# Three maximum units in a row behind the transposed scores: a change to the order of TensorE's work in the first attention

## The chip, the cores and the metric

The kernel runs on one core of a Trainium2 chip. The metric is the device time of one execution in microseconds; the time before is the median of three runs, 1740.41 us. A profile comes from one further execution, which took 1746.19 us and whose instructions span 1744.5 us.

## The reference

The program computes two transformer layers in sequence, each an attention and a mixture of experts behind layer norms with residual adds. All values are float32. Only the first attention bears on the change. Cut to what matters:

```python
# z: (2, 1024, 128), 16 heads of 64
q = z @ wq @ fcq_w + fcq_b
k = z @ wk @ fck_w + fck_b
v = z @ wv @ fcv_w + fcv_b
scores = einsum('bihd,bjhd->bhij', q, k) / 8
attn = softmax(scores, axis=-1)      # over all 1024 keys
out = einsum('bhij,bjhd->bihd', attn, v)
return out.reshape(b, n, 1024) @ fco_w + fco_b
```

For each of 2 x 16 heads there are 1024 x 1024 scores; the softmax takes a maximum over the keys of each query, an exponential, and a sum.

## The kernel before

The first attention (`l0_attention`) works through 16 steps. A step is one pair of heads of one batch element, with all its 1024 queries and keys. It loops over 8 key tiles of 128 keys (kt 0 to 7). For each key tile TensorE computes the transposed scores, with keys on the partitions and queries along the free axis, in two blocks of 512 queries: `("ST", kt, 0)` and `("ST", kt, 1)`. Each is 4 matmuls (lines 683 and 684, two per head, into one PSUM pair). ScalarE takes the exponential of each pair into a `prob` tile (line 550). GpSimd adds the `prob` tiles up over kt into `psum_k` (lines 502 and 507). TensorE multiplies the `prob` tiles with the values and accumulates in PSUM over kt: `("PV", kt - 1, j)`, one key tile behind the scores (line 656, 4 matmuls per block j, 8 for both).

The maxima that a step subtracts are found one step ahead. For step n + 1 TensorE also computes plain scores with queries on the partitions, in 16 units `("s", x)`: unit x takes query tile x // 2 and half x % 2 of the keys, for both heads (lines 629 and 631, two matmuls that sit in different row groups of the array). VectorE reduces each such pair to its row maxima (line 571). After the sixteenth, VectorE joins the two halves (`mmax`, line 575), unit `m` transposes the result on TensorE (line 635), VectorE makes a row of it (line 580), and SyncE moves it by DMA into the operand `q2` of the next step.

Other units: `q` projects the next step's queries (line 620, read on ScalarE, line 517, and VectorE, line 565). `l`, `r`, `n` and `g` finish the step before: `l` sums `psum_k` over partitions on TensorE (line 640; VectorE copies it out on line 584), `r` is a reciprocal on VectorE (line 587) whose result goes out by DMA and comes back spread over the partitions as `rb`, `n` is the product `on` of `ut` and `rb` on VectorE (line 591), and `g` is the output projection on TensorE (line 645) with an add on VectorE behind it (line 595).

The order is written out by hand. `step_script(n)` makes one list, and every engine walks it:

```python
for kt in range(TT):
    out += [("ST", kt, 0), ("ST", kt, 1)]
    out += [("UNIT",) + u for u in AFTER_SCORES.get(kt, []) if u in has]
    if kt or n:
        out += [("PV", kt - 1, 0), ("PV", kt - 1, 1)]
    out += [("UNIT",) + u for u in AFTER_VALUES.get(kt, []) if u in has]
```

PSUM holds two banks for the accumulating `pv` and a ring of three pairs (`RING = 3`, two banks each). Every ST block and every unit but `r` and `n` takes the next pair of the ring in the order of the script; PV takes none. Before TensorE writes a pair it waits for the reader of the tile three places back in that order, either the exponential (semaphore `exp_done`) or the reading unit (`read`):

```python
def await_buffer(pe, kind, at):
    i = turn[(kind, at)]
    if i >= RING:
        before, count = tiles[i - RING]
        pe.wait_ge(exp_done if before == "ST" else read, count + 1)
```

So in an ordinary key tile the ring goes ST 0, ST 1, s, s, s, and the reader that each waits for is that of, in turn, the last tile's first s, its second s, its third s, this tile's ST 0 and this tile's ST 1. The instructions of an engine run in their order in the script. The sixteenth step has no next one and so no `q`, `s` or `m` units; the sixteen units for the first step run ahead of the loop.

Of the kernel before, what the change touches and what calls it, by code (L numbers as in the profile page):

```python
# [302 lines left out]
def step_units(k_next, k_done):  # L303
# [5 lines left out]

AFTER_SCORES = {  # L310
    0: [("q", 0), ("q", 1)],
    1: [("s", 0), ("s", 1)], 2: [("s", 3), ("s", 4)], 3: [("s", 6), ("s", 7)], 4: [("s", 9), ("s", 10)],
    5: [("s", 12), ("s", 13)], 6: [("s", 15)],
}
AFTER_VALUES = {
    1: [("s", 2), ("l", 0)], 2: [("s", 5)], 3: [("s", 8), ("r", 0)], 4: [("s", 11), ("n", 0)], 5: [("s", 14), ("g", 0)],
    6: [("m", 0)],
}


# [1765 lines left out]
```

## Time and profile before

| | |
|---|---|
| median of 3 runs | 1740.41 us (1734.69 to 1742.39) |
| the profiled execution | 1746.19 us, span 1744.5 us |
| TensorE matmul busy | 1435.8 us (82%) |
| VectorE busy | 997.7 us (57%) |
| ScalarE busy | 795.7 us (46%) |
| GpSimd busy | 899.7 us (52%) |

The steps of the first attention lie between about 109 and 835 us of the span. In the views, PE is TensorE's matmul, PEld its weight load, DVE VectorE, ACT ScalarE, POOL GpSimd and SP SyncE. A line of the timeline gives the start, the duration, the engine and line, the operation, what it writes and reads with the shapes, and how many instructions are merged; in brackets stands the idle time of the engine before it and what ended it. Matmuls are pipelined, so the next one's start says more than a duration does.

### The profile page before, as it was taken

The page shows a single profiled execution, that of the slowest core. Times are in us where ns is not written, and L with a number is a line of the kernel's source. Part 1 is how long each engine was busy: PE and PEld are TensorE (multiplying, and loading weights), DVE is VectorE, ACT ScalarE, POOL GpSimd, SP SyncE. Part 2 cuts the span into 40 slices and gives each one's busy share as a digit, 9 for nine tenths or more (in the row PEclk, how much of TensorE's full clock was granted, in tenths as well). Part 3 has the DMA queues.
Part 4 walks back from the last instruction along what each step waited for, and adds up shares of the span by engine and source line. Part 5 has one row for each costly group of instructions (what it writes and reads, how often), then busy time and mean ns, then how long its engine had stood idle before and what let it go on. Part 6 is the DMA issues. An engine that isn't in the chain of part 4 may idle for free. (4 is left out here: it accounts for less than half of the span.)

```text
span 1744.5 us, 19190 instructions
## 1 busy us (share of the span) xinstructions
PE 1435.8 (82%) x6318; PEld 816.1 (47%) x6318; DVE 997.7 (57%) x1646; ACT 795.7 (46%) x1152; POOL 899.7 (52%) x703
## 2 busy tenths in 40 slices
PE   4679999999999999996458646988788885399998
PEld 3534444444444444442336423444344443277776
DVE  3165666666665656651635556655455514488777
ACT  2224444444443434432225342555455463388787
POOL 0227777777776767787225322445444232054444
PEclk9579999999999999998579887998889886599999
DMA  3000000000000000000144122111211102402200
GB/s 78 4 1 2 14 14 14 14 14 14 14 13 14 14 13 14 14 14 25 37 98 96 58 69 53 25 25 38 55 32 25 26 3 109 86 13 49 60 6 6
DMA packets 34562, 55.28 MB, mean 32 GB/s; under 512 B 10009, under 2 KB 15522, under 8 KB 33762
## 3 DMA queue, kind: packets, MB, share of 16 engines
q1 hardware_dynamic: 34482, 54.26, 12.5%
q8 instruction: 44, 0.72, 0.2%
q14 instruction: 36, 0.29, 0.1%
HBM read 37.73 MB, written 1.44 MB: 22 GB/s over the span
## 5 line engine op out<-in xcount | busy, mean ns | idle before, releaser
L507 POOL TENSOR_TENSOR psum_k<-psum_k,prob 128x1024 f32<-128x1024 f32 x192 | 463.3, 2436 | 85.5 <-ACT prob L550 85.5
L550 ACT ACTIVATE prob<-pair 128x1024 f32<-128x1024 f32 x256 | 251.3, 1027 | 422.0 <-PE pair L684 421.8
L571 DVE TENSOR_REDUCE mx<-pair 128x2 f32<-128x1024 f32 x256 | 303.9, 1221 | 114.6 <-PE pair L631 114.6
L1611 DVE CUSTOM_DVE_ANT_0 l_banks<-l_banks,causal 128x128 f32<-128x128 f32 (+7 forms) x256 | 189.9, 781 | 147.9 <-PE l_banks L1640 146.5
L656 PE MATMUL pv<-prob,c_all 128*64 128x512 f32 x1024 | 247.7, 605 | 0.0
L1527 ACT ACTIVATE l_prob<-l_banks 128x1024 f32<-128x1024 f32 (+7 forms) x256 | 156.3, 655 | 169.1 <-PE l_banks L1659 169.0
L683 PE MATMUL pair<-qq,ak 128*128 128x512 f32 x512 | 223.0, 436 | 5.6 <-DMA q<-scratch_shift 4.6
L684 PE MATMUL pair<-q,kb 128*128 128x512 f32 x512 | 204.5, 399 | 0.0
L1804 POOL TENSOR_TENSOR silu_rest<-silu,silu_lead 128x512 fp32r<-128x512 f32 x72 | 113.1, 1570 | 150.6 <-ACT silu_lead L1848 150.6
L1640 PE MATMUL l_banks<-l_kk,l_qq 128*128 128x512 f32 (+3 forms) x384 | 126.7, 424 | 70.6 <-DMA l_qq<-l_head 65.3
L1573 POOL TENSOR_SCALAR_AFFINE_SELECT l_prob<-l_prob 128x128 f32<-128x128 f32 x256 | 71.7, 295 | 192.2 <-ACT l_prob L1527 191.1
L1876 DVE TENSOR_TENSOR silu<-silu,gb 128x512 f32<-128x512 f32 x128 | 139.2, 1089 | 27.7 <-ACT silu L1855 25.7
L1640 PEld LDWEIGHTS l_banks<-l_kk,l_qq 128*128 128x128 f32 x384 | 75.2, 222 | 135.5 <-issue 90.8
L683 PEld LDWEIGHTS pair<-qq,ak 128*128 128x128 f32 x512 | 97.5, 190 | 83.5 <-issue 32.5
L502 POOL TENSOR_TENSOR psum_k<-prob 128x1024 f32<-128x1024 f32 x32 | 75.4, 2377 | 112.9 <-ACT prob L550 112.9
L1659 PE MATMUL l_banks<-l_qq,l_kk 128*128 128x512 f32 (+3 forms) x384 | 122.1, 410 | 4.2 <-DVE l_mx L1611 3.6
L629 PE MATMUL pair<-ak,qq 64*128 64x512 f32 x256 | 112.4, 486 | 6.2 <-DVE mx L571 5.3
L565 DVE SCALAR_TENSOR_TENSOR q<-pair,q_bias,qq 64x512 fp32r<-64x512 f32 x64 | 44.4, 759 | 125.1 <-ACT qq L517 125.1
L656 PEld LDWEIGHTS pv<-prob,c_all 128*64 128x64 f32 x1024 | 62.2, 136 | 109.1 <-issue 77.7
L631 PE MATMUL pair<-kb,qq 64*128 64x512 f32 x256 | 112.4, 486 | 0.0
L684 PEld LDWEIGHTS pair<-q,kb 128*128 128x128 f32 x512 | 97.8, 191 | 22.2 <-issue 4.1
L1848 ACT CAST silu_lead<-silu 128x512 fp32r<-128x512 f32 x144 | 88.9, 620 | 28.8 <-DVE silu L1876 28.8
(221 smaller groups left out, 2265.6 us busy)
## 6 DMA issues: line engine op xcount, KB each, us to landing
gb<-scratch_gates SPq DMA_DIRECT2D x8, 2048.0 KB, 14.1
rb<-scratch_sums SPq DMA_DIRECT2D x32, 256.0 KB
l_qq<-qr SPq DMA_DIRECT2D x8, 768.0 KB, 5.6
whole_r<-in_w SPq DMA_DIRECT2D x2, 2304.0 KB, 11.4
l_kk<-l_head SPq DMA_DIRECT2D x64, 64.0 KB, 2.0
l_qq<-l_head SPq DMA_DIRECT2D x64, 64.0 KB, 2.0
x<-in_x SPq DMA_DIRECT2D x4, 256.0 KB, 6.6
whole_r<-in_up SPq DMA_DIRECT2D x1, 1024.0 KB, 5.2
```

The source lines that it names most:

```text
L507: nc.gpsimd.tensor_tensor(total[:, h, :], total[:, h, :], prob[kt % 4][:, h, :], ALU.add).then_inc(summed, 1)
L550: nc.scalar.activation(prob[kt % 4][:, :, ts(j, BLK)], buffer("ST", at)[:, :, :], ACT.Exp, scale=D0 ** -0.5).then_inc(exp_done, 1)
L571: nc.vector.reduce_max(mx[:, x % 2, :, x // 2], buf[:, :, :], AX.X).then_inc(read, 1)
L656: ins = nc.tensor.matmul(pv[D0 * h:D0 * (h + 1), ts(j, BLK)], m.c_all[:, TT * (s // PAIRS) + kt, :], prob[kt % 4][:, h, ts(j, BLK)], start ...
L683: nc.tensor.matmul(buf, m.ak[:, keys], qq[n % 2][h][:, ts(j, BLK)], start=True, stop=False)
L684: ins = nc.tensor.matmul(buf, m.kb[:, keys], q2[n % 2][h][:, ts(j, BLK)], start=False, stop=True)
L1527: nc.scalar.activation(prob[kt % 2][:, g, P * kt:T], buffer(item)[:, P * kt - T:], ACT.Exp, scale=SCALE1).then_inc(exp_done, 1)
L1611: ins = nc.vector.tensor_tensor_reduce(scores[:, 0:s_width(t)], scores[:, 0:s_width(t)], hidden, 1.0, -3e38, ALU.add, ALU.max, mx[:, g, t: ...
L1640: ins = nc.tensor.matmul(out[:, lo:end], qq[k % 2][:, g, ts(t, P)], kk[k % 2][:, g, lo:end], start=True, stop=True)
L1659: ins = nc.tensor.matmul(buf[:, at:at + end - lo], kk[n % 2][:, g, ts(kt, P)], qq[n % 2][:, g, lo:end], start=True, stop=True)
L1804: engine.tensor_tensor(rest[u % R][:, :], s[u % R][:, :], lead[u % R][:, :], ALU.subtract).then_inc(rest_done[u % 2], 1)
L1876: nc.vector.tensor_tensor(s[u % R][:, :], s[u % R][:, :], m.gb[:, j % 2, u // CH, :], ALU.mult).then_inc(gated, 1)
```

## The change

For key tiles 1 to 5 the third maximum unit, which stood behind the two PV blocks, now stands ahead of them, right behind the other two. Key tile 6 keeps its single unit. The rank of every unit and every ST block among themselves stays as it was, and so do the ring's places and the orders of ScalarE, VectorE, GpSimd and SyncE: only on TensorE do two `PV` blocks and one `s` unit change places.

```diff
 AFTER_SCORES = {
     0: [("q", 0), ("q", 1)],
-    1: [("s", 0), ("s", 1)], 2: [("s", 3), ("s", 4)], 3: [("s", 6), ("s", 7)], 4: [("s", 9), ("s", 10)],
-    5: [("s", 12), ("s", 13)], 6: [("s", 15)],
+    1: [("s", 0), ("s", 1), ("s", 2)], 2: [("s", 3), ("s", 4), ("s", 5)], 3: [("s", 6), ("s", 7), ("s", 8)],
+    4: [("s", 9), ("s", 10), ("s", 11)], 5: [("s", 12), ("s", 13), ("s", 14)], 6: [("s", 15)],
 }
 AFTER_VALUES = {
-    1: [("s", 2), ("l", 0)], 2: [("s", 5)], 3: [("s", 8), ("r", 0)], 4: [("s", 11), ("n", 0)], 5: [("s", 14), ("g", 0)],
-    6: [("m", 0)],
+    1: [("l", 0)], 3: [("r", 0)], 4: [("n", 0)], 5: [("g", 0)], 6: [("m", 0)],
 }
```

## Rows read from the trace of the kernel before

**Rows 1.** Busy time per engine in one step; after the counts PEclk, DMA share, GB/s.

```profile
345.00:389.00 44.00, 42.51 (x185) 20.85 (x184) 27.32 (x27) 18.97 (x22) 33.76 (x15) 1.00 0.05 13
```

**Rows 2.** The timeline of one ordinary key tile (kt 3 of a step).

```profile
300.02 0.50 PE L683 MATMUL pair<-qq,ak 128*128 128x512 f32 x1
...
301.25 1.96 ACT L550 ACTIVATE prob<-pair 128x1024 f32<-128x1024 f32 x2 [3.08 <-PE pair L684]
...
302.08 0.49 PE L629 MATMUL pair<-ak,qq 64*128 64x512 f32 x1
...
302.33 0.18 PEld L629 LDWEIGHTS pair<-ak,qq 64*128 64x128 f32 x1
...
302.42 0.41 PE L629 MATMUL pair<-ak,qq 64*128 64x512 f32 x1
...
302.62 2.36 DVE L571 TENSOR_REDUCE mx<-pair 128x2 f32<-128x1024 f32 x2 [1.26 <-PE pair L631]
...
302.77 1.94 PE L656 MATMUL pv<-prob,c_all 128*64 128x512 f32 x8
...
303.29 4.73 POOL L507 TENSOR_TENSOR psum_k<-psum_k,prob 128x1024 f32<-128x1024 f32 x2 [0.31 <-ACT prob L550]
...
304.63 0.49 PE L629 MATMUL pair<-ak,qq 64*128 64x512 f32 x1
...
305.06 0.50 PE L683 MATMUL pair<-qq,ak 128*128 128x512 f32 x1
```

**Rows 3.** The costliest groups of the page: the exponentials.

```profile
L550 ACT ACTIVATE prob<-pair 128x1024 f32<-128x1024 f32 x256 | 251.3, 1027 | 422.0 <-PE pair L684 421.8
```

**Rows 4.** Timeline, end of a step: a single s, PV behind it, m, PV, ST.

```profile
363.14 0.49 PE L629 MATMUL pair<-ak,qq 64*128 64x512 f32 x1
...
363.56 1.94 PE L656 MATMUL pv<-prob,c_all 128*64 128x512 f32 x8
...
366.86 0.38 PE L635 MATMUL pair<-ident,mmax 128*16 128x128 f32 x2 [1.36 <-DVE mmax L575]
...
369.23 1.94 PE L656 MATMUL pv<-prob,c_all 128*64 128x512 f32 x8
...
371.10 0.50 PE L683 MATMUL pair<-qq,ak 128*128 128x512 f32 x1
```

**Rows 5.** Timeline, key tiles 4 and 5 of a usual step: r, n, g.

```profile
350.45 0.25 DVE L587 RECIPROCAL inv_c<-sums_c 128x16 f32<-128x16 f32 x1
...
354.12 0.50 PE L683 MATMUL pair<-qq,ak 128*128 128x512 f32 x1
...
356.69 1.48 DVE L591 TENSOR_TENSOR on<-ut,rb 128x1024 f32<-128x1024 f32 x1 [1.24 <-DMA rb<-scratch_sums]
...
358.09 3.47 DVE L571 TENSOR_REDUCE mx<-pair 128x2 f32<-128x1024 f32 x3
...
359.36 1.98 PE L645 MATMUL pair<-on,g_all 128*128 128x512 f32 x4
...
360.78 0.79 PE L683 MATMUL pair<-qq,ak 128*128 128x512 f32 x1
```

**Rows 6.** Timeline, key tile 5 of another step, where `rb` lands late.

```profile
530.07 0.50 PE L683 MATMUL pair<-qq,ak 128*128 128x512 f32 x1
...
534.11 2.67 DVE L591 TENSOR_TENSOR on<-ut,rb 128x1024 f32<-128x1024 f32 x1 [2.70 <-DMA rb<-scratch_sums]
...
537.97 2.42 PE L645 MATMUL pair<-on,g_all 128*128 128x512 f32 x4 [2.79 <-DVE mx L571]
539.40 1.42 PE L683 MATMUL pair<-qq,ak 128*128 128x512 f32 x1
...
541.47 0.63 PE L684 MATMUL pair<-q,kb 128*128 128x512 f32 x1
...
547.37 0.50 PE L683 MATMUL pair<-qq,ak 128*128 128x512 f32 x1
```

**Rows 7.** Waits of TensorE's matmuls, 100 to 780 us: total, times, longest.

```profile
PE pair L645 <- DVE mx L571: 5.8, 3, 2.8
```

## The prediction

> **What bounds the kernel now.** I looked first at the busy time per engine in stretches. Over one whole step of the first attention TensorE's matmuls are busy for 42.51 of 44.00 us at a granted clock of 1.00, with GpSimd at 33.76 and VectorE at 27.32 [rows 1]. So in this stage the time is the sum of what TensorE does in order, and the change touches only that order. Then I read the timeline of one ordinary key tile from its first score matmul to the next tile's [rows 2]: ST at 300.02, the first s at 302.08 (2.06 later), the second at 302.42 (0.34), PV at 302.77 (0.35), the third s at 304.63 (1.86), the next ST at 305.06 (0.43). That is 5.04 us, and TensorE waits for nobody in it. The reader should see what else is placed in that row of times: the two exponentials begin at 301.25 and last 1.96 together, so the first is over at 301.25 + 1.03 = 302.28 (1027 ns each, [rows 3]) and the second at 303.21. The second s's weight load starts at 302.33, 0.05 after the first exponential's end. That is the ring at work: the second s writes the pair that the first ST block filled, so it may start only when that block's exponential is done, and here it just about can.
>
> **The change part by part.**
>
> *The third s waits for the second exponential.* The third s takes the pair of the second ST block (three places back in the ring), and the edit doesn't alter that. In the old place it came at 304.63, 1.42 us after the exponential's end at 303.21, so the wait never showed. In the new place TensorE would reach it one s behind the second, at 302.42 + 0.34 = 302.76, while its pair is free only at 303.21. With the 0.05 us of release seen at the second s it starts at 303.26: a stall of 0.50 us in each such tile. The exponential can't come sooner, since it hangs on the last of the eight ST matmuls, which is ahead of all this, and ScalarE stood idle 3.08 us before the first one. Queued behind the waiting s on TensorE are both PV blocks, any `l` or `g`, and the next ST, so all of the stall goes into the period.
>
> *The joins.* An s that starts after a break takes 0.42 until PV starts (363.14 to 363.56, [rows 4]); one that follows another s takes 0.35 [rows 2]. I take 0.42, since this one starts after a break. PV to the next ST takes 1.87 (369.23 to 371.10, [rows 4]). So the new period is 3.24 to the third s (300.02 to 303.26), 0.42, and 1.87: 5.53 to 5.54 us against 5.04, or +0.50. The old s-to-ST join of 0.43 is gone in this, else it would be +0.93. The bounds of this term: if the third s needn't wait, the tile would take 2.06 + 0.34 + 0.34 + 0.35 + 1.87 = 4.96, a gain of 0.08; if after the stall the weight load of 0.18 [rows 2] had to be over before the matmul starts, it is +0.68. I take the value of the second s, which waits for the same kind of event.
>
> *How often.* Steps 0 to 14 have units for a next step, 5 such tiles each: 75. Tile 1 has `l` behind the third s; it moves behind PV and its joins change in the same way, so it counts as ordinary. Tile 5 has `g` there and is counted apart: 14 times (step 0 has no `g`). That leaves 61 tiles at +0.50 = +30.5 us.
>
> *Tile 5 with g.* It takes 6.66 us now (354.12 to 360.78), of which 1.42 from g to the next ST [rows 5]. g there starts just as the first of three reductions that began at 358.09 ends (358.09 + 1.22 = 359.31): g's pair is the one that the first s of the tile used, and VectorE reads that late, because the product `on` stands before it and had waited for `rb`. In the new order: third s at 3.24, PV 0.42 later, g 1.87 later, at 5.53, next ST 1.42 later: 6.95, so +0.30 if g doesn't wait. To see whether it waits, I follow `rb`. It is asked for by the reciprocal, which now starts 1.37 into tile 4 (350.45; tile 4 began 5.04 before 354.12) as it follows the third s's reduction. With the third s filled at 3.24 + 0.49 = 3.73, VectorE is still at the second (302.62 + 2.36 is 4.96 into the tile), so the third reduction ends near 4.96 + 1.2 = 6.1, 0.6 into the next tile. From the reciprocal to `on` are 356.69 - 350.45 = 6.24 us, so `on` can start 0.6 + 6.24 - 5.54 = 1.3 into tile 5 and not 2.57. GpSimd's adds start when both exponentials are done (303.29, 3.27 into a tile, 4.73 for the two [rows 2]) and so end 2.46 into the next. If `on` must wait for these it ends at about 2.46 + 1.1 = 3.6, and the first reduction at 4.8, before g at 5.53. Good for no wait in g either way: 14 x 0.30 = +4.2.
>
> Here the row shows `on` lasting 1.48 and 2.67 us for the same work, according to where GpSimd's adds stood [rows 5, 6]. The Trainium skill (SBUF — State Buffer, "Who interferes with whom") says that a VectorE instruction with two SBUF inputs contends with a GpSimd instruction that reads SBUF, and that the later one is fully blocked; the trace agrees, as 1.48 and 2.67 show. By that rule `on` ends at 3.6, without it at 2.6; the sum is the same.
>
> *What late `rb` costs now.* In two of the fourteen steps `rb` came late: `on` started 4.04 into the tile (530.07 to 534.11), took 2.67, and g waited 2.79 us for the reduction [rows 6]; the three waits of 5.8 us in all with the longest at 2.8 say that another step had the same [rows 7]. The tile took 9.33 instead of 6.66 and the one up to 547.37 took 7.97 where a usual one takes 6.39 (ST matmuls of 0.63 instead of 0.40: the clock had fallen behind the stall). That is 4.25 us each time. In the new order the same lateness (7.71 from reciprocal to `on`) puts `on` at 0.6 + 7.71 - 5.54 = 2.8, its end near 3.9 and the reduction near 5.1: still before g. So the new order takes these stalls away where they occur: -8.5 us in the profiled execution, 0 where none occurred.
>
> *Edits at nothing.* VectorE has three reductions in a row, but their ends at 3.8, 5.0 and 6.1 after the tile's start stand against the next tile's first ST at 5.5, its second ST at about 6.5 and its first s at 7.6, which want these pairs back: 1.5 us of cover for each. PV is 0.9 us later in its tile; who waits for it is the exponential that reuses `prob` four tiles on, some 17 us later. `l` is read 0.5 us later; its DMA and the reciprocal lie two tiles apart. Tiles 6, 7 and 0 keep their order: tile 6's wait of 1.36 us before m [rows 4] comes from VectorE's `mmax` behind the lone s, and is the same distance from the tile's start.
>
> **Sum.** +30.5 + 4.2 - 8.5 = +26.2 on the profiled execution's 1746.2 us: 1772.4. That execution lies 5.8 us above the median of the runs shown, about what one or two late `rb` make; the runs spread over 7.7 us, as two such would. A run with none of them would be 1746.2 - 8.5 = 1737.7, and with the 34.7 us on it 1772; from the lowest run, 1734.7, it is 1769. I take 1771 us, 1.8% slower.
>
> **Rivals.**
>
> *Not slower: the third s doesn't wait.* The tile becomes 4.96: 61 x -0.08 = -5, tile 5 loses its small g wait, about 0.3 x 14 = -4, and the late `rb` cost up to 8.5 less. From the median that is about 1728 us. It decides from the point where the second exponential is over by 302.7 rather than 303.21. For it speaks only that a few ends of matmuls are modelled; against it, that the second s starts 0.05 behind its own exponential. Chance 0.03.
>
> *The stalls bring the clock down.* Behind the 2.79 us stall the ST matmuls ran 0.63 instead of 0.40, the lower of the two levels [rows 6]. If 75 new breaks of 0.5 us did that for one tile in each of 15 steps, a tile's work at half speed would take some 9 us instead of 5.5: +52 us, 1824. Against it: fifteen breaks of 1.36 us before m are there already, and the step with one of them has a granted clock of 1.00 [rows 1, 4]. Chance 0.04. The Trainium skill (TensorE: Matmul & The Clock Gate, "A second HAM failure mode: psum-queue depth-cycling") warns of just this, that short idles between groups of matmuls make the clock go up and down; no row here shows it for breaks under 1.4 us.
>
> *`on` falls badly against GpSimd.* Its start moves to a new phase of the adds. If it had to wait for the next pair of adds as well (to 3.27 + 2.37 = 5.6, end at 6.7, reduction at 7.9), g would wait 2.4 us and, as in the late steps, the clock could fall: up to 14 x 4 = +56, 1827. Against it: GpSimd stands idle 0.8 us from 2.46 to 3.27 in the new tile, and `on` waits from before that. Chance 0.04.
>
> *Smaller than forecast.* The 0.50 us is partly taken in by joins that I can't see (an s after s could take less than 0.34, or the exponential's end come a tenth sooner): +0.35 a tile, about 1761. Chance 0.14, inside or at the edge of the range.
>
> **Numbers.** The forecast itself has 0.75. The range of 1762 to 1782 holds about +0.40 to +0.65 a tile and the 0 to 2 late `rb`. This kernel's measurement can tell about 0.5% (9 us) from no change. Slower by more than that: 0.94; the same: 0.03; faster: 0.03.
>
> **What would show it.** In the changed profile a tile 2, 3 or 4 lasts 5.54 us; TensorE (or its weight load) sits idle before the third s with the exponential of line 550 as what ended it, about 0.5 us, 75 times; PV follows 0.42 later and ST 1.87 after PV; tile 5 lasts 6.95 with no wait of g for a reduction; no ST matmuls of 0.63 in steps 1 to 14; `on` starts about 1.3 into tile 5; m still waits 1.36. The prediction is wrong if the tile keeps 5.04 or less, or if the granted clock falls below 1.00 in the steps.

## The result, and the profile after

The changed kernel takes 1767.32 us (median of 4 runs, 1764.76 to 1768.65) where the one before takes 1739.62 us (median of 4). The ratio is 1.0161 with a 95% interval of [1.0134, 1.0188]: 27.7 us or 1.6% slower (23 to 33 us by the interval). The forecast was 1771 us with a range of 1762 to 1782. The profiled execution took 1768.65 us against 1746.19 before, 22.5 us more; the working had it at 1772.4.

The waits of the changed kernel come first (engine, what it writes and its line, what it waited for, total us, times, longest; all line numbers are one less than before). The first two rows had no counterpart in the kernel before.

```profile
PEld pair L628 <- ACT prob L549: 55.7, 75, 0.8
...
PE pair L628 <- ACT prob L549: 31.9, 75, 0.4
...
PE pair L634 <- DVE mmax L574: 23.4, 16, 2.9
```

Seventy-five times, in all five tiles of fifteen steps, the matmuls of an s unit stand idle for 0.43 us until an exponential ends. The place is plain in the timeline of a key tile 4, which answers to the ordinary tile of before [rows 2]:

```profile
313.73 0.50 PE L682 MATMUL pair<-qq,ak 128*128 128x512 f32 x1
...
314.97 1.95 ACT L549 ACTIVATE prob<-pair 128x1024 f32<-128x1024 f32 x2 [3.59 <-PE pair L683]
...
315.79 0.50 PE L628 MATMUL pair<-ak,qq 64*128 64x512 f32 x1
...
316.13 0.41 PE L628 MATMUL pair<-ak,qq 64*128 64x512 f32 x1
316.34 3.49 DVE L570 TENSOR_REDUCE mx<-pair 128x2 f32<-128x1024 f32 x3 [1.77 <-PE pair L630]
...
316.98 0.49 PE L628 MATMUL pair<-ak,qq 64*128 64x512 f32 x1 [0.43 <-ACT prob L549]
...
317.40 1.94 PE L655 MATMUL pv<-prob,c_all 128*64 128x512 f32 x8
...
319.27 0.49 PE L682 MATMUL pair<-qq,ak 128*128 128x512 f32 x1
```

The two exponentials are over at 314.97 + 1.95 = 316.92, the third s starts 0.06 later, PV 0.42 after it and the next ST 1.87 after PV: 5.54 us for the tile, where the one before took 5.04. Two key tiles 5 follow. The first is a usual one; the second belongs to the step in which `rb` had landed late before [rows 6], and it lands late here as well (`on` starts 2.79 into the tile).

```profile
320.73 2.06 DVE L590 TENSOR_TENSOR on<-ut,rb 128x1024 f32<-128x1024 f32 x1 [0.90 <-DMA rb<-scratch_sums]
...
322.71 3.47 DVE L570 TENSOR_REDUCE mx<-pair 128x2 f32<-128x1024 f32 x3
...
324.81 1.98 PE L644 MATMUL pair<-on,g_all 128*128 128x512 f32 x4
326.23 0.80 PE L682 MATMUL pair<-qq,ak 128*128 128x512 f32 x1
...
550.79 0.49 PE L682 MATMUL pair<-qq,ak 128*128 128x512 f32 x1
...
553.58 1.23 DVE L590 TENSOR_TENSOR on<-ut,rb 128x1024 f32<-128x1024 f32 x1 [2.24 <-DMA rb<-scratch_sums]
...
554.73 3.48 DVE L570 TENSOR_REDUCE mx<-pair 128x2 f32<-128x1024 f32 x3
...
556.33 1.98 PE L644 MATMUL pair<-on,g_all 128*128 128x512 f32 x4
557.75 0.80 PE L682 MATMUL pair<-qq,ak 128*128 128x512 f32 x1
```

Both tiles last 6.96 us (319.27 to 326.23 and 550.79 to 557.75), and g waits for no reduction in either. Before, they lasted 6.66 and 9.33. The granted clock over a step is still full:

```profile
320.00:366.00 46.00, 42.31 (x181) 20.40 (x181) 27.33 (x26) 18.93 (x22) 32.55 (x15) 1.00 0.05 12
```

TensorE is busy for about as long as in a step before (42.3 us against 42.5 [rows 1]), but a step takes 46.3 us and not 44.0.

### The profile page after: what moved, and what is told of

It reads as the page before. It is cut to its first block and busy times, and to the rows that moved or that the text cites. A ratio compares the mean times of both kernels' runs of the same rounds, so it can differ in the third digit from the quotient of the medians.

```text
span 1766.9 us, 19190 instructions
## 1 busy us (share of the span) xinstructions
PE 1435.9 (81%) x6318; PEld 812.3 (46%) x6318; DVE 1000.7 (57%) x1646; ACT 794.6 (45%) x1152; POOL 890.1 (50%) x703
## 5 line engine op out<-in xcount | busy, mean ns | idle before, releaser
L506 POOL TENSOR_TENSOR psum_k<-psum_k,prob 128x1024 f32<-128x1024 f32 x192 | 454.4, 2389 | 120.5 <-ACT prob L549 120.5
L570 DVE TENSOR_REDUCE mx<-pair 128x2 f32<-128x1024 f32 x256 | 298.1, 1218 | 129.3 <-PE pair L630 129.3
```

Of the source, the lines that this page charges most:

```text
L506: nc.gpsimd.tensor_tensor(total[:, h, :], total[:, h, :], prob[kt % 4][:, h, :], ALU.add).then_inc(summed, 1)
L570: nc.vector.reduce_max(mx[:, x % 2, :, x // 2], buf[:, :, :], AX.X).then_inc(read, 1)
```

## The experiments

The eight were timed in two series, each beside the kernel before on one chip: the first four (before: 1738.74 us), and on another chip the last four (before: 1736.13 us). Theory A throughout is that of the prediction: the ring makes the third s wait for the exponential of the second ST block.

**The third s between the two PV blocks.** It keeps the unit in front of half of PV, but behind the exponential.

```diff
-            out += [("PV", kt - 1, 0), ("PV", kt - 1, 1)]
+            out += [("PV", kt - 1, 0)]
+            out += [("UNIT",) + u for u in BETWEEN_VALUES.get(kt, []) if u in has]
+            out += [("PV", kt - 1, 1)]
```

> The third s stands between the two PV blocks. Theory A (the third s must wait for the exponential of the second ST block, over 3.20 us into the tile): TensorE gets to it at 2.06 + 0.34 + 0.35 + 0.93 = 3.68, so the wait is hidden again, and a tile lasts 3.68 + 0.43 + 0.94 = 5.05 us; time within 0.3% of the kernel before, near 1740 us. Rival B (it is PV coming later, and the next ST right behind PV, that costs; or s to PV joins): one more join s to PV and PV to s stands here, so the tile would be 5.2 to 5.5 us and the time 1752 to 1765 us.

Measured: 1747.03 us, ratio 1.0050 [1.0035, 1.0065]. A key tile 4 of this kernel, whose line numbers are two more than those of before:

```profile
308.43 0.50 PE L685 MATMUL pair<-qq,ak 128*128 128x512 f32 x1
...
311.17 1.08 PE L658 MATMUL pv<-prob,c_all 128*64 128x512 f32 x4
...
312.18 0.49 PE L631 MATMUL pair<-ak,qq 64*128 64x512 f32 x1
...
312.61 1.08 PE L658 MATMUL pv<-prob,c_all 128*64 128x512 f32 x4
...
313.61 0.50 PE L685 MATMUL pair<-qq,ak 128*128 128x512 f32 x1
```

No matmul of an s unit waits for an exponential here, so that part of theory A holds. But the tile is 5.19 us and not 5.05. Half of PV takes 1.01 us until what follows it (311.17 to 312.18), not half of 1.87: each half pays anew what a run of eight pays once, 0.15 us a tile. So neither forecast came out whole. Theory A had the wait right and the tile and the time (near 1740 us) too low; rival B's range for the tile begins where the measured one lies (5.2), but its 1752 to 1765 us did not come. This run alone doesn't decide between them; the next one does.

**A shorter exponential.** The changed kernel, but of the second ST block only half of the columns are exponentiated, so that its output isn't a softmax. The `memset` instructions and ScalarE's wait for them are left out of the cut below.

```diff
-nc.scalar.activation(prob[kt % 4][:, :, ts(j, BLK)], buffer("ST", at)[:, :, :], ACT.Exp, ...)
+w = BLK if j == 0 else BLK // 2
+nc.scalar.activation(prob[kt % 4][:, :, ds(BLK * j, w)], buffer("ST", at)[:, :, 0:w], ACT.Exp, ...)
```

> The changed kernel, but the exponential of the second ST block of every key tile takes only half of its columns (the other half of prob keeps ones, set before the steps; four memsets on GpSimd delay the start of the steps by some microseconds, so the tiles are to be read and not only the total). Theory A: that exponential lasts about 0.65 us instead of 1.03, the third s starts about 0.35 us sooner, at 2.85 to 2.91 into the tile instead of 3.25, and the tile lasts 5.15 to 5.21 us instead of 5.54; the whole is about 26 us less than the changed kernel, less the start, 1743 to 1752 us. Rival B: TensorE's order alone costs the 0.50, the tile stays at 5.54 and the time at or above 1767 us.

Measured: 1741.31 us, ratio to the kernel before 1.0026 [1.0009, 1.0043]. A key tile 4 of it (line numbers four more than before):

```profile
309.11 0.49 PE L687 MATMUL pair<-qq,ak 128*128 128x512 f32 x1
...
310.34 1.52 ACT L554 ACTIVATE prob<-pair 128x1024 f32<-128x1024 f32 x2 [3.58 <-PE pair L688]
...
311.50 0.42 PE L633 MATMUL pair<-ak,qq 64*128 64x512 f32 x1
...
311.92 0.18 PEld L633 LDWEIGHTS pair<-ak,qq 64*128 64x128 f32 x1 [0.31 <-ACT prob L554]
...
314.22 0.49 PE L687 MATMUL pair<-qq,ak 128*128 128x512 f32 x1
```

The two exponentials last 1.52 together instead of 1.95, 0.43 less (the expectation had about 0.38). They end at 311.86, the weight load of the third s starts at 311.92, 2.81 into the tile, and the tile is 5.11 us, 0.43 less than 5.54. The tile follows the exponential one to one. TensorE's order is the same as in the changed kernel, so the order alone isn't what costs.

The total, 26.0 us under the changed kernel's median, equals the expected "about 26 us" by luck; the time lies just under the expected 1743 to 1752. Between the two traces the steps save 34.2 us: 0.43 in each of the 75 tiles and 0.42 in each of fifteen tiles 6, less some 4 us for one late `rb` in step 9. The steps also start 6.9 us later, behind the `memset` instructions.

**One tile alone.** The kernel before with only tile 2 changed.

```diff
-2: [("s", 3), ("s", 4)]          # AFTER_SCORES
+2: [("s", 3), ("s", 4), ("s", 5)]
-2: [("s", 5)],                   # AFTER_VALUES
```

> Only key tile 2 has its third s ahead of PV. Theory A, a price per tile: tile 2 lasts 5.54 us and the others 5.04, so 15 x 0.50 = 7.5 us, near 1747 us (ratio 1.004), and late rb still costs where it occurs. Rival B (the cost builds up through VectorE's backlog over tiles in a row): tile 2 alone would cost less than 0.2 us, under 3 us in all.

Measured: 1746.02 us, ratio 1.0052 [1.0034, 1.0071], which is 6 to 12 us. The third s and the next ST of such a tile, which began at 296.33:

```profile
296.33 0.51 PE L683 MATMUL pair<-qq,ak 128*128 128x512 f32 x1
...
299.58 0.49 PE L629 MATMUL pair<-ak,qq 64*128 64x512 f32 x1 [0.43 <-ACT prob L550]
300.00 1.94 PE L656 MATMUL pv<-prob,c_all 128*64 128x512 f32 x8
301.87 0.49 PE L683 MATMUL pair<-qq,ak 128*128 128x512 f32 x1
```

5.54 us, while tile 1 ahead of it lasts 6.04 and tile 3 behind it 5.04, both as before: the full price in one tile with no others around it. Nothing builds up, and rival B is out. A late `rb` still costs in this kernel: tile 5 of step 9 lasts 10.69 us.

**All three behind PV.** This tests the other side of the ring.

```diff
-    1: [("s", 0), ("s", 1), ("s", 2)], 2: [("s", 3), ("s", 4), ("s", 5)], ...   # AFTER_SCORES
+    1: [("s", 0), ("s", 1), ("s", 2), ("l", 0)], 2: [("s", 3), ("s", 4), ("s", 5)], ...   # AFTER_VALUES
```

> All three s units of tiles 1 to 5 stand behind PV. No s waits for an exponential then (both are over at 3.20, the first s comes at 2.06 + 1.87 = 3.93). If three in a row cost nothing as such: tile 3.93 + 0.34 + 0.34 + 0.43 = 5.03, time near 1740 us. By the ring and VectorE: the first reduction starts at 4.47 and ends at 5.69, the next ST wants that pair at 5.04 and so starts at 5.74; the tile is 5.7 us, 75 x 0.7 = 50 us more, and reductions on the path make g wait too: 1790 to 1805 us.

Measured: 1802.52 us, ratio 1.0374 [1.0341, 1.0406]. The waits of its TensorE matmuls:

```profile
PE pair L682 <- DVE mx L570: 40.3, 47, 0.9
...
PE pair L644 <- DVE mx L570: 14.2, 14, 3.0
PE pair L639 <- DVE mx L570: 12.0, 14, 0.9
```

A tile lasts 5.94 to 5.96 us (one begins at 324.23 in the timeline, the next at 330.19), 0.25 more than expected. The first ST block waits 0.86 for a reduction, and the second one waits too. In this tile its weight load is held up:

```profile
325.36 0.19 PEld L682 LDWEIGHTS pair<-qq,ak 128*128 128x128 f32 x1 [0.37 <-DVE mx L570]
```

With that PV starts 2.27 into the tile (326.50) instead of 2.06, and all that follows is later by as much. So three s in a row lose ahead of PV by the exponential and behind it by VectorE. With two ahead and one behind, as before, each of the three pairs has been read by the time it is wanted; so it has with the third between the PV blocks. One ahead and two behind was not tried.

**The reciprocal a tile earlier.** This and the next test the two terms beside the ring: the late `rb`, and the wait before m.

```diff
-    1: [("s", 2), ("l", 0)], 2: [("s", 5)], 3: [("s", 8), ("r", 0)], ...
+    1: [("s", 2), ("l", 0)], 2: [("s", 5), ("r", 0)], 3: [("s", 8)], ...
```

> The kernel before with the reciprocal r one key tile earlier (behind the third s of tile 2 instead of tile 3), so rb lands some 5 us earlier. Theory A (step 9, and at times step 11, pay about 4.25 us each for a late rb): on starts about 1.4 us into tile 5 in every step, no tile 5 lasts over 6.8 us, no ST matmul of 0.63; the time falls by 4 to 9 us, near 1733 us. Tile 5 keeps 6.66 where on still waits for GpSimd's adds (to 2.97, end 4.05). Rival: the stalls of steps 9 and 11 are not from rb and stay; the time is the same within 2 us.

Measured: 1732.41 us, ratio 0.9978 [0.9963, 0.9993]. No matmul of g waits for a reduction any more, every tile 5 of steps 1 to 14 lasts 6.63 us, that of step 9 (counted from 0) too, and behind none of them does an ST matmul last 0.63. Tile 5 of step 9, where `rb` had been late:

```profile
527.93 0.50 PE L683 MATMUL pair<-qq,ak 128*128 128x512 f32 x1
...
529.18 2.77 DVE L591 TENSOR_TENSOR on<-ut,rb 128x1024 f32<-128x1024 f32 x1
531.20 5.30 POOL L507 TENSOR_TENSOR psum_k<-psum_k,prob 128x1024 f32<-128x1024 f32 x2 [0.34 <-ACT prob L550]
531.87 3.47 DVE L571 TENSOR_REDUCE mx<-pair 128x2 f32<-128x1024 f32 x3
533.14 1.98 PE L645 MATMUL pair<-on,g_all 128*128 128x512 f32 x4
534.56 0.80 PE L683 MATMUL pair<-qq,ak 128*128 128x512 f32 x1
```

The medians differ by 3.7 us (1 to 6 by the interval), just under the expected 4 to 9. The stalls were from `rb`, since nothing but the place of `r` was changed. From one profiled execution to the other the steps take 8.5 us less (688.3 against 696.8), the price of the two stalls; by the medians a run without a profile loses 3.7 to late `rb`, nearer to one stall than to two. Why `rb` is late, and in step 9 of six of the ten traces here, stays open.

**The maximum of the halves as a reduction.**

```diff
-nc.vector.tensor_tensor(mmax[:, :, :], mx[:, 0, :, :], mx[:, 1, :, :], ALU.max)
+nc.vector.reduce_max(mmax[:, :, :], mx[:, :, :, :].rearrange("p a h t -> p h t a"), AX.X)
```

> The kernel before with mmax as a reduction over the two halves of mx (one input) instead of a tensor_tensor of two SBUF inputs. Theory A (mmax lasts 1.78 us because it waits for GpSimd's add, not for its 16 columns): it lasts under 0.3 us, m follows PV without the 1.36 wait, tile 6 lasts about 4.97 us instead of 6.40, 15 x 1.4 = 21 us less, near 1718 us. Rival (mmax is slow in itself, or the next step's rows come late by the same amount): tile 6 stays above 6 us, or tile 0 of the next step starts later by 1.4.

Measured: 1718.71 us, ratio 0.9884 [0.9860, 0.9908]. Tile 6 of a step, which began at 310.98:

```profile
314.56 4.70 POOL L507 TENSOR_TENSOR psum_k<-psum_k,prob 128x1024 f32<-128x1024 f32 x2 [1.63 <-ACT prob L550]
315.15 0.19 DVE L575 TENSOR_REDUCE mmax<-mx 128x16 f32<-128x32 f32 x1
315.64 0.39 PE L635 MATMUL pair<-ident,mmax 128*16 128x128 f32 x2
315.97 0.50 PE L683 MATMUL pair<-qq,ak 128*128 128x512 f32 x1
```

The same 16 results take 0.19 us instead of 1.78, m no longer waits, and tile 6 lasts 4.99 us instead of 6.40: 15 x 1.4 = 21 us by the tiles, 17.4 by the medians, 16 to 24 by the interval.

That the two-input form isn't slow in itself, two other lines show. The first is from the kernel before, ahead of the loop, where GpSimd has no add to run; the second is from the kernel with the shorter exponential, where GpSimd's adds begin and end 0.43 us sooner:

```profile
104.41 0.18 DVE L575 TENSOR_TENSOR mmax<-mx 128x16 f32<-128x16 f32 x1
...
368.65 1.36 DVE L579 TENSOR_TENSOR mmax<-mx 128x16 f32<-128x16 f32 x1
```

The same instruction lasts 0.18 us with no add beside it, 1.78 in the kernel before and 1.36 where the add ends sooner. In all the tiles 6 of both traces it ends about 0.03 us after the add does.

**Both edits, and both with three in a row.** The fourth of the series puts the two edits on the changed kernel.

> The kernel before with both edits, r earlier and mmax as a reduction. If the two are apart from one another: 25 to 30 us less than before, 1709 to 1714 us. Rival: GpSimd's adds now follow each other without a pause and something of the gain goes into a wait of the exponentials or of l for the sums: less than 20 us in all.

> The changed kernel (three s units ahead of PV) with both edits. By the prediction's terms three in a row costs 61 x 0.50 + 14 x 0.30 = 34.7 us where no rb is late, against 26 to 28 us where one or two are. So this should lie 34 to 35 us above e7_both, near 1746 us. If late rb was no part of the balance it lies 27 to 28 us above.

Measured: 1710.33 us for the kernel before with both, ratio 0.9855 [0.9832, 0.9879]; 1747.06 us for the changed kernel with both, ratio 1.0059 [1.0037, 1.0081]. The first is 25.8 us under the kernel before, as expected from two gains that don't touch, and the fastest of all here; the rival of under 20 us is out. The second lies 36.7 us above it (32 to 40, an estimate from the spread of their six and seven runs), where the plain pair differs by 27.7. From the first ST matmul of the steps to the first of the last key tile the two traces differ by 35.0 us (701.9 against 666.9); for the plain pair it is 25.7 (722.4 against 696.8). Where no `rb` stall is there to be taken away, three in a row costs what the tiles say, 34.7 by the prediction's sum; the 27 to 28 of the other case is out.

```profile
PE pair L628 <- ACT prob L549: 31.9, 75, 0.4
```

In its waits the row of the exponential is the very one of the changed kernel, and none is left for a reduction.

## Why the prediction was right

*The third s waits for the second exponential.* Right in place, cause and size. Forecast 0.50 a tile and a tile of 5.54; measured 5.54. From the second s to the third are 0.85 us (316.13 to 316.98), 0.51 more than the 0.34 without a wait; the row of waits has 0.43, as it counts from the end of the second s. The shorter exponential shows the cause, since the tile moves by the 0.43 that the exponential moves; the single tile shows that it is a price per tile.

*The joins.* Right: 0.42 from a late s to PV, 1.87 from PV to ST, or to g.

*Tile 5.* Forecast 6.95, measured 6.96. `on` was forecast to start 1.3 into the tile and starts at 1.16 to 1.64 in the steps with a usual `rb`; forecast to end at 3.6, it ends at 3.5 (320.73 + 2.06, less 319.27).

*Late rb.* Forecast: the same lateness would put `on` at 2.8 and no longer hold up g. It was late in the same step again, at 2.79, and g did not wait. In the changed kernel's trace only step 9 shows it, and step 11, the other one of before, is usual. The two steps had taken 48.3 and 48.4 us instead of 44.0; they now take 46.35 and 46.3, as the others. So the new order is seen to take one late `rb` without a stall, in step 9. In step 11 nothing was late this time, so that half of the 8.5 us is the chance of one execution.

*Sum.* In the steps themselves it is +25.7 us in the profiled execution against a forecast of +26.2. Term by term, tile against tile, the two traces give +30.3 for the 61 tiles (forecast +30.5), +4.2 for the fourteen tiles 5 with the stalls set aside (+4.2), -8.5 for the stalls (-8.5), and -0.3 for the other tiles. The whole execution differs by 22.5 only, since the time up to the first ST matmul is 2.0 us less (107.5 against 109.5) and that behind the last tile 1.2 less (937.0 against 938.2); the edit touches neither, so I take both for spread. The medians differ by 27.7, between the sum for two late `rb` (26.2) and for none (34.7); one would make 30.5. How often `rb` is late in a run without a profile is not counted anywhere. The kernel with the reciprocal a tile earlier gives an estimate: late `rb` cost 3.7 us a run there (1 to 6), which would make 34.7 - 3.7 = 31 (28 to 34). The measured difference, 23 to 33 by its interval, lies under the 34.7 of no stall but can't tell one stall from two, and that is what stays open of the sum.

*Rivals.* The clock did not fall behind the 75 new breaks. `on` did not have to wait for a second pair of adds. The weight load of the third s did not add its 0.18. One rival was argued wrongly: "smaller than forecast" named an s that follows an s in less than 0.34. That brings TensorE to the third s sooner but not the third s itself, which starts when the exponential ends, so it can't shorten the tile.

*One term was taken too large.* The bound of "no wait" and the stall of 0.50 took 0.34 for a third s behind the second. The kernel with all three behind PV shows it where no s waits:

```profile
328.36 0.50 PE L628 MATMUL pair<-ak,qq 64*128 64x512 f32 x1
...
328.70 0.39 PE L628 MATMUL pair<-ak,qq 64*128 64x512 f32 x1
...
328.94 0.39 PE L628 MATMUL pair<-ak,qq 64*128 64x512 f32 x1
```

0.34 to the second, but 0.24 to the third. If the same holds behind ST as here behind PV, which no run shows, TensorE could have been at the third s 0.1 us sooner and loses 0.6 there rather than 0.5; a tile without the wait would have been 2.06 + 0.34 + 0.24 + 0.35 + 1.87 = 4.86, a gain of 0.18 and not 0.08. The forecast went by the exponential's end and not by this, so it was untouched; the rival on the faster side would have been worth about 8 us more (75 x 0.1).

## What to carry to other kernels

When buffers in PSUM go round in a ring of three, reordering work on TensorE moves each unit against the reader of the tile three places back. Write down, for every unit, when that reader ends and when the unit would start; here four numbers of one tile gave the new length of the tile. A wait that shows in no list may be hidden with a margin of nothing (the second s) or of 1.4 us (the third), and a unit may be moved up by no more than its margin: the third s was moved up by the 1.87 us of PV. And a 16-column instruction that lasts 1.8 us is worth a question before any reordering: that one edit gained 1.2%.

## What the runs showed of the hardware that was not expected

The two VectorE instructions with two SBUF inputs beside GpSimd's adds, `on` and `mmax`, ended at the same moment wherever they started. In the changed kernel `on` starts anywhere from 1.16 to 1.64 into tile 5 and ends at 3.52 (the late one apart); with both edits it starts at 0.47, lasts 3.05 and ends at 3.52 again. GpSimd's add ends at 2.44 in both. With `rb` early in the kernel before, `on` lasts 2.77 us from 1.25 to 4.02, and the add ends at 2.94. Its own work is 1.23 (the late one at 553.58, which started while GpSimd was idle). The rest is the wait for GpSimd's running add, and GpSimd's next pair of adds is stretched from 4.7 to 5.3 in return. The Trainium skill (SBUF — State Buffer, "Who interferes with whom") says that such an instruction contends with GpSimd's reads and a reduction does not; the trace agrees, as `mmax` at 1.78 against 0.19 us shows.

A change between these kinds of matmul is not free. Inside a run of ST matmuls one starts every 0.23 us; from the last of them to the first s it is 0.33, from a late s to PV 0.42, and half of a PV run takes 1.01 instead of 0.93. In the kernel that splits PV the 61 ordinary tiles are 0.15 us longer each (9.2 us); the fourteen tiles 5 are not, at 6.62 us against 6.66. That makes 8.6 us, and the medians differ by 8.3.

Breaks of 0.43 us in every 5.54 left the granted clock at 1.00, as did the fifteen of 1.36 and, with all three s behind PV, the 74 of 0.86. The Trainium skill (TensorE: Matmul & The Clock Gate, "A second HAM failure mode: psum-queue depth-cycling") warns that short idles between groups bring it down; at these lengths the trace doesn't agree. The stalls of 2.79 us before g were followed by ST matmuls of 0.63 [rows 6]. But a longer one was not: with all three s behind PV, g stood for 3.01 us until 676.90, and the ST matmuls behind it last 0.40. The granted clock (third number from the end) of ten microseconds around a stall, in the kernel before and in this one:

```profile
538.00:548.00 10.00, 8.64 (x27) 4.50 (x28) 6.68 (x6) 2.05 (x2) 4.44 (x3) 0.83 0.00 0
674.00:684.00 10.00, 6.15 (x22) 2.87 (x22) 8.97 (x7) 1.97 (x2) 6.01 (x3) 1.00 0.00 0
```

Of seven stalls of 2.3 to 3.0 us before g in the traces here, six saw the clock fall to its lower level, in the stall or within 1.5 us of its end; this one did not. What decides it stays open.
